# A scan layer followed by experts: one more of the products with C moved from VectorE to GpSimd

## The reference, cut to what matters

```python
x_dbl = jnp.einsum('ke,bel->bkl', x_proj_w, u)
dt_lo = x_dbl[:, :DR]
Bm = x_dbl[:, DR:DR + DS]
Cm = x_dbl[:, DR + DS:]
delta = jax.nn.softplus(jnp.einsum('er,brl->bel', dt_proj_w, dt_lo) + dt_proj_b[None, :, None])
A = -jnp.exp(A_log)

def step(state, xs):
    d_t, B_t, C_t, u_t = xs
    dA = jnp.exp(d_t[..., None] * A)
    state = state * dA + (d_t * u_t)[..., None] * B_t[:, None, :]
    y_t = jnp.einsum('ben,bn->be', state, C_t)
    return (state, y_t)
...
y = y + D[None, :, None] * u
y = y * jax.nn.silu(z)
```

## Time and profile before

| | us |
|---|---|
| runs of the kernel, median (lowest to highest) of 3 | 1278.87 (1272.02 to 1279.64) |
| the execution that was profiled | 1277.93 |
| its span, from the first to the last instruction | 1276.0 |
| first scan starts, last unit's sum is ready | 41.5, 536.3 |
| busy in the whole span: PE, DVE, POOL, ACT | 1132.7, 755.7, 632.6, 527.9 |

### The profile page before, as it was taken

One profiled execution on the slowest core, in us unless ns is written; L12 is line 12 of the kernel. 1 busy time (PEld: TensorE's weight loads), 2 busy tenths in 40 slices (PEclk: granted clock), 3 DMA queues, 4 the chain that ended last, 5 costly groups with the idle time before them and its releaser, 6 DMA issues.

```text
span 1276.0 us, 19356 instructions
## 1 busy us (share of the span) xinstructions
PE 1132.7 (89%) x4944; PEld 843.3 (66%) x4944; DVE 755.7 (59%) x823; ACT 527.9 (41%) x705; POOL 632.6 (50%) x467
## 2 busy tenths in 40 slices
PE   6686988698868888847999999999999999999996
PEld 2344554457444647546788888888888888888885
DVE  5888999897979899756324353532432435314321
ACT  5856757674767464213223142321321323213210
POOL 0798999898979999304222232222321322223211
PEclk9687777776868667557999999999999999999998
DMA  6453254524452445074314253421421534315211
GB/s 202 152 140 106 86 139 120 160 79 127 114 157 83 132 114 151 0 263 165 108 41 166 107 181 109 168 104 49 176 96 41 181 109 164 106 49 181 95 37 42
DMA packets 70373, 153.21 MB, mean 120 GB/s; under 512 B 8911, under 2 KB 15055, under 8 KB 70337
## 3 DMA queue, kind: packets, MB, share of 16 engines
q1 hardware_dynamic: 56368, 116.34, 26.9%
q0 software_dynamic: 13968, 36.45, 10.5%
HBM read 320.80 MB, written 18.35 MB: 266 GB/s over the span
## 4 chain that ended last, share of the span: by engine, by line
PE 53%; DVE 2%; issue 1%; DMA 1%; ACT 0%; POOL 0%; POOLq 0%; DVEq 0%; ACTq 0%
PE hp L1549 11%; PE hp L1547 11%; PE hp L1548 11%; PE yp L1549 5%; PE yp L1547 5%; PE yp L1548 5%; PE tp L1589 2%; PE xp L1541 1%; PE yp L1594 0%; DVE R L1385 0%; DMA work<-out_dram,acc_index 0%; DMA out_dram<-work,out_index 0%; DVE S_tok L1381 0%; DVE S_w L1376 0%; DVE S_w L1489 0%
## 5 line engine op out<-in xcount | busy, mean ns | idle before, releaser
L297 POOL TENSOR_TENSOR ring<-du,bB 128x1024 f32<-128x1024 f32 x128 | 310.6, 2499 | 38.5 <-DVE du L694 37.6
L625 DVE TENSOR_TENSOR_SCAN ring<-dA,ring 128x512 f32<-128x512 f32 x256 | 295.9, 1204 | 16.3 <-ACT dA L393 14.4
L393 ACT ACTIVATE dA<-delta,Acol 128x512 f32<-128x512 f32 x256 | 174.8, 689 | 165.0 <-DVE ring L625 163.3
L1547 PE MATMUL hp<-w_hi,xT_hi 128*128 128x512 f32 x592 | 237.6, 401 | 2.3 <-DVE xT_lo L1444 1.4
L1549 PE MATMUL hp<-w_hi,xT_lo 128*128 128x512 f32 x592 | 235.7, 398 | 0.0
L1548 PE MATMUL hp<-w_lo,xT_hi 128*128 128x512 f32 x592 | 233.8, 395 | 0.0
L791 PEld LDWEIGHTS yT<-ident,ring 128*128 128x128 f32 x1024 | 144.9, 171 | 132.9 <-issue 55.5
L1188 POOL DMA_INDIRECT out_dram<-work,out_index x37 | 37.6, 1017 | 376.2 <-DVE work L1451 369.6
L791 PE MATMUL yT<-ident,ring 128*128 128x128 f32 x1024 | 173.8, 330 | 44.4 <-POOL ring L306 25.4
L1465 DVE TENSOR_TENSOR work<-hp,work 128x512 f32<-128x512 f32 x74 | 51.1, 690 | 238.4 <-PE hp L1549 238.4
L1422 DVE TENSOR_TENSOR w_lo<-stage,w_hi 128x2048 fp32r<-128x2048 f32 x48 | 109.0, 2288 | 38.7 <-ACT w_hi L1232 38.5
(11 more groups left out here) (203 smaller groups left out, 1326.4 us busy)
## 6 DMA issues: line engine op xcount, KB each, us to landing
stage<-in_L_ffn_w_kernel_dram SPq DMA_DIRECT2D x160, 1024.0 KB
stage<-in_L_ffn_wo_kernel_dram SPq DMA_DIRECT2D x78, 1024.0 KB
bB<-bcs SPq DMA_DIRECT2D x64, 512.0 KB, 3.6
bC<-bcs SPq DMA_DIRECT2D x40, 256.0 KB, 4.4
xall<-in_x_dram SPq DMA_DIRECT2D x1, 4096.0 KB, 13.8
xln_dram<-xlnb SPq DMA_DIRECT2D x4, 1024.0 KB, 6.9
out_dram<-xall SPq DMA_DIRECT2D x4, 1024.0 KB, 9.0
xall<-g POOLq DMA_DIRECT2D x7, 512.0 KB, 5.6
```

What stands on the lines that cost most here:

```text
L297: g_.tensor_tensor(ring[:, q % RING, :].rearrange("p (e l) -> p e l", e=2), dub(b, h * 2 * L, 2 * L).rearrange("p (e l) -> p e l", e=2), B ...
L393: a_.activation(dA[r % SB][:, :], db(b, eb * L, L), ACT.Exp, scale=Acol[:, eb, n:n + 1]).then_inc(exp_done, 1)
L625: v_.tensor_tensor_scan(o, dA[r % SB][:, :], o, 0.0, ALU.mult, ALU.add).then_inc(scan_done, 1)
L1547: t_.matmul(bank[:, :], a_hi[:, k, :], b_hi[:, b, :], start=(start and k == ks[0]), stop=False)
```

## The change

State 0 joins the states whose product with C GpSimd makes. DVE has ten of sixteen left, and TensorE fills C for those ten.

```diff
-POOL_C = (2, 5, 8, 11, 14)
+POOL_C = (0, 2, 5, 8, 11, 14)
```

## The result

The changed kernel took 1279.15 us (median of 19 runs, 1277.51 to 1282.46). The kernel before, run beside it, took 1272.16 us (19 runs, 1266.75 to 1279.64). The ratio is 1.0041, with a 95% interval from 1.0023 to 1.0059, which is 2.9 to 7.5 us. (A ratio here is not the quotient of the two medians, which would be 1.0055.) So the time was forecast 1.9 us too high, within the 1% that had a chance of 0.83, and the sign of the small difference was right.

What follows compares the result with a forecast made beforehand. No engine's load was taken as the bound, but the chain of waits at each place: 1.0 (start) + 0.4 (batch 1) + 1.8 (last half) = 3.2 us on the profiled 1277.93, so 1281 us, range 1272 to 1289.

Steps and rivals of the forecast that it cites:

- Not a matter of throughput: Whole units' stage: engine shares decide nothing; what a product is worth depends on where it stands.
- The bounds of -9.0 and +18.6 us: All eight halves as pure throughput: 9.0 us off DVE at one end, 18.6 us onto POOL at the other.
- Second halves, 0: Batches 0 to 2: ACT's exp sets unit 18's scan, DVE's wait grows to 3.40 us, POOL's wait absorbs 2.32: 0.
- First halves of batches 1 to 3, 0.4 us: New product lies off the chain, POOL's waits absorb it; only batch 1's later `add_y` delays `stats_2`: 0.4 us, bounds 0 and 1.
- The start, 1.0 us: Batch 0: POOL's product of unit 0 delays unit 5's input and unit 2's product; 1.0 us lost, bounds -1.3 and +2.
- the upper bound's case: Start of batch 0: fillings of units 3 and 4, behind a later `acc(0)`, come at the low clock: +2.
- The last half, 1.8 us: Batch 3: POOL's later product of unit 117 delays `acc` and `logits_of`; 1.8 us lost, bounds 1.5 and 2.7.
- The waits: Sign of being right: DVE's total waits grow by about 12 us, POOL's before L306 fall from 37.2 to about 24.
- the 506.4 named as a sign: Last half: `logits_of` starts near 506.4 us if the forecast is right.
- Rival 1: POOL becomes the bound between units 36 and 66, 2.32 us per half: 1296.5 us if all count; chance 0.10 above 1291.
- Rival 2: DVE is the bound and gets all eight products' time back: 1269 us; chance 0.10 for 1266 to 1273.
- Rival 3: TensorE's clock falls otherwise, one chain moving 3 to 4 us: 1275 or 1289 us; chance 0.2, equal for both sides.

Runs made afterwards that it cites:

- e2_middle: The kernel before with state 0's product moved to POOL only in the six halves between the first and last: 1277.77 us, ratio 1.0015.
- e5_early_add: The changed kernel with `add_y` of a batch's second half issued at s == 6 instead of 8: 1278.60 us, ratio 1.0016 to the kernel before.
- e1_ends: The kernel before with state 0's product moved to POOL only in the first and last halves: 1276.29 us, ratio 0.9996.
- e9: The kernel before with state 14 on DVE and state 0 on POOL at three batch changes, fillings after POOL units issued earlier: 1257.80 us, ratio 0.9865.
- e10: The kernel before with only the fillings that follow a POOL unit issued one step earlier on TensorE: 1257.70 us, ratio 0.9893.
- e4_after: The changed kernel measured once more, in a second set beside the kernel before: 1281.11 us, ratio 1.0034.
- e8_busy: The kernel before with the fillings of units 32, 64 and 96 done four times, to keep TensorE busy: 1274.55 us, ratio 0.9999.
- e7_only14: The kernel before with state 14 moved from POOL to DVE at three batch changes, nothing put in its place: 1268.50 us, ratio 0.9944.

## Why the prediction was right, step by step

- **Not a matter of throughput: right.** The bounds of -9.0 and +18.6 us were both refuted, in the whole (+3.05 us between the traces, +2.9 to +7.5 by the runs) and by e2_middle. The forecast of the difference, 3.2 us, lies at the low end of that interval; the forecast of the time came so near because its base was a profiled execution of 1277.93 us, 5.8 above the median of the 19 runs of before.
- **Second halves, 0: right** in size and in form: 3.39 us of wait against 3.40, POOL's wait at unit 18 down to 1.85 where 1.1 was left by the sum (the new delay of DVE gave it more), no change of the shift at the places themselves (units 16 to 20, 48 to 52, 80 to 84: 0.1 us at most).
- **First halves of batches 1 to 3, 0.4 us: right, at 0.2.** POOL's lateness was absorbed where forecast; the product of unit 50 waited 0.29 us (0.03 forecast), that of unit 104 0.52. The path through `add_y` is the one forecast. What no step had is the 2.3 us that the clock gave DVE in between; they were lost in the wait for `add_y`; the trace of e5_early_add, which issues it earlier, is 2.0 to 2.4 us ahead of the changed kernel's from unit 69 on.
- **The start, 1.0 us: the place right, the size within its bounds.** The input of unit 5 began at 55.72 us (55.75 forecast). The rows below show what the step left out: `loss` took 2.23 us where it takes 1.20 alone, since POOL now had a product at that time (2.23 us in the traces of all five kernels that have unit 0 on POOL, 1.20 in the nine others), and the fillings behind `acc(0)` came at the low clock, the upper bound's case. The shift was +0.5 us at unit 8 and +1.7 at unit 15. The unchanged kernel itself moved by -1.2 and -0.3 there, so no finer split is earned.

The start of the changed kernel, POOL, DVE and TensorE in turn, the places of the earlier trace rows:

```profile
50.69 2.34 POOL L306 TENSOR_TENSOR ring<-ring,bC 128x1024 f32<-128x1024 f32 x1
53.00 1.20 POOL L267 TENSOR_TENSOR rs<-rs 128x16 f32<-128x16 f32 x1
...
55.72 4.66 POOL L297 TENSOR_TENSOR ring<-du,bB 128x1024 f32<-128x1024 f32 x2
...
51.88 2.23 DVE L648 SCALAR_TENSOR_TENSOR du<-spw,spy 128x1024 f32<-128x1024 f32 x1
...
53.09 1.97 PE L791 MATMUL yT<-ident,ring 128*128 128x128 f32 x8 [5.70 <-POOL ring L306]
```

- **The last half, 1.8 us: the mis-sized term.** The mechanism was right: POOL's product of unit 117, then `acc`, then `logits_of`. The delay was 3.1 us at unit 123, since `logits_of` came wholly at the low clock (6.83 us instead of 5.88). It was then given back entirely (3.1 us), by a rise of the clock at a time that did not move with the work. So this half cost 0 between the traces. That the sum still came out at 3.4 against 3.2 is luck: 1.7 by unit 20, 0.8 at unit 21, 0.2 at the change of batch, 0.6 in small steps until unit 85 and 0.1 behind it. Of these the unchanged kernel, profiled again, shows the 0.8 as 0.7 and the 0.6 as 0.5.
- **The waits: near.** DVE +9.5 us (12 forecast), POOL's L306 26.5 (24 forecast). `logits_of` of the last half started at 508.74 us, 2.3 later than the 506.4 named as a sign: 3.4 us had arrived there instead of 1.4, and its own delay was 2.1 instead of 1.8.
- **Rival 1 (POOL the bound)** had 0.10 and fell. **Rival 2 (DVE gains)** fell. **Rival 3 (clock)** was right as a source of error: in the traces it moved things by 0.5 to 3 us at the start, in batch 1 and in the last half, with both signs. In the medians it may be more: none of the 31 runs of the changed kernel and none of the 12 of e5_early_add lies below 1275 us, where of e1_ends five of twelve do and of the kernel before 20 of 74. Which step of the change shuts those times off wasn't found: no execution below 1275 us of these kernels was profiled.

## What to carry to other kernels

That two engines are equally busy says nothing of what a piece of work costs on either; ask for each place which wait ends last behind it. Here eight moved products cost 3 us between the traces (3 to 7 by the medians), while three others of the same kind, at a change of batch, were worth 9 to 12 us by the medians, part of it the clock's and `loss`'s, since there TensorE's `acc` waited for just those on POOL. On the base with earlier fillings the same three were worth nothing that shows (e9 against e10): a price holds for the chain in which it was read. And an instruction whose inputs are long ready, such as a filling, belongs in its queue ahead of those that have to wait: an edit of three lines took the median from 1276.24 to 1257.70 us.

## What the runs showed of the hardware

**A DVE instruction can be held for as long as POOL has work in a row.** `loss` (L648) has both inputs in SBUF. Its eight executions in e4_after, minimum, median and maximum in ns:

```profile
L648 DVE SCALAR_TENSOR_TENSOR du<-spw,spy x8: 1214/2550/10228, 32.6 to 437.1; 128x1024 f32<-128x1024 f32 x8
```

and in the kernel before:

```profile
L648 DVE SCALAR_TENSOR_TENSOR du<-spw,spy x8: 1199/2071/3295, 32.8 to 429.3; 128x1024 f32<-128x1024 f32 x8
```

The three long ones, 8.53, 8.53 and 10.23 us, each ended 1.1 to 1.2 us behind the start of POOL's next DMA issue. So did one of 8.19 us in e9_swap_early's profiled run (1264.24 us, against 1256.92 to 1258.15 in four others), one of 5.16 in e8_busy and one of 4.70 in e7_only14. The Trainium skill ("SBUF — State Buffer", section "Who interferes with whom") says that a DVE instruction with two SBUF inputs contends with a GpSimd instruction that reads SBUF, and calls the shared ports an exclusive lock; of DVE's two-port modes it says that whoever issues first has them for the whole instruction while the other blocks fully. The trace agrees that `loss` blocks, but here it stayed blocked over three to four POOL instructions. The lengths near 2.5 us in all runs would be a wait for one; that wasn't tested. The change puts one more product into such rows of POOL's, which fits the two runs of e4_after at 1288 and 1290 us; that they come from it is shown for the first alone.

**TensorE stayed at its low level while busy without a gap.** In the last half all 27.0 of 27.0 us were busy, with the clock share at 0.50, 1.2 of 2.4 GHz (second row of the first fence here; before it was 30.5 of 30.5 in the earlier trace rows). The Trainium skill ("TensorE: Matmul & The Clock Gate", section "What's actually happening") says that activity releases the throttle. These rows differ from that for as long as they last: TensorE was active for all of the 27.0 us, and the clock stayed low. In e8_busy it was busy for all 11.04 us from 291.36 to 302.40 us, with the clock share at 0.50 too.
